# Graph-network kernel on one core: the first chunk's one-hot matrices built gather by gather, and the second chunk begun in half columns

## The chip, the cores and the metric

The kernel runs on one core of one Trainium2 chip. The metric is the device time of one execution, in microseconds; the kernel before takes 249.6 us (median of 3 runs, 249.52 to 250.2). The profiled execution is a fourth run with a time of its own.

## The reference, cut to what matters

1250 nodes with 512 features, 21250 edges sorted by destination. What the change touches is the first sum over neighbours (`segment_sum`); all that follows reads its result.

```
agg = jax.ops.segment_sum(x[src], dst, num_segments=N)
h = (1.0 + eps) * x + agg                      # first graph layer
h = relu(batch_norm(h @ W1 + b1, g1, be1))
h = relu(batch_norm(h @ W2 + b2, g2, be2))
x = layernorm(x + (x + h))
h = relu(x @ lW1 + lb1) @ lW2 + lb2            # second graph layer
x = layernorm(x + (h + segment_sum(h[col], row)))
```

## The kernel before

**Tiling.** The sum over neighbours is a matrix product with a count matrix `AT` (source node on the partitions, in 10 tiles `k` of 128 rows; destination node along 1250 columns). Features stand in 4 tiles `d` of 128. The columns are cut into three chunks `CH`: 0 to 250, 250 to 750 and 750 to 1250. A *unit* `(i, k)` is the pair of matmuls that adds source tile `k` of feature tile `d` to chunk `c` (`i = 4 c + d`): one for the high part `xh` of x, one for the remainder `xl = x - xh`, 250 columns wide in the first chunk and 500 in the others. A result `i` stays in PSUM bank `2 + i % 6` until ten units have gone into it.

**How AT is made.** Edges are packed as `dst * 1280 + src` (`pair`, VectorE), written to DRAM (`pairs`) and read back by two indirect DMAs that GpSimd issues one after the other: `run0` holds for each of 125 windows of 10 nodes the edges of its first five nodes, `run1` those of its last five. Where each window begins is its rank, found from `below` and `edge_row` on VectorE and four matmuls. VectorE subtracts the window's base (`rel`), TensorE transposes (L1182), and VectorE splits the result in `keyT` (source tile and node) and `loT` (source row in the tile). From these it makes, for each of 25 *groups* `g` of 50 columns, two one-hot matrices `hot_s` and `hot_k` (`one_hots`, L849 and L852, two buffers each). TensorE multiplies them in `build(g)` (ten matmuls of 50 columns, L1200, banks 0 and 1), and ScalarE copies the bank to `AT` (`group_out`, L569). `build(g)` needs the one-hots of g and the copy of g-2; the one-hots of g need `build(g-2)` done.

**The order of work.** Every engine runs an order written out by hand and waits on semaphores. The first five groups (`EARLY`) come ahead of everything; then groups 5 to 24 are *slots*: in slot g TensorE runs `build(g)` and the units that `slot_units[g]` lists (four in each). Slots 5 to 14 hold the 40 units of the first chunk, slots 15 to 24 the 40 of the second; the third chunk's 40 (`tail_units`) follow. Tables tell in which slot an engine does other things, on VectorE and ScalarE behind the one-hots or the copy of that slot:
- `cols_at` (TensorE): transposes of x tile k (`x_cols`), four matmuls. `turn_at` (ScalarE): their copy to `xT` (`x_turn`).
- `high_at` (ScalarE): `xh` of tile k (`x_high`, L565). `low_at` (VectorE): `xl` of tile k (`x_low`, L828), which waits for that `xh`.
- For a result that is done, VectorE adds `(1 + eps) x` two slots later (`h0_own`, L863), ScalarE rounds it three slots later (`h0_high`), and VectorE takes the remainder five slots later (`h0_low`, L870).

`between(n)` issues n matmuls of 256 columns whose result nobody reads.

## Time and profile before

| | before |
|---|---|
| Time, median of 3 runs | 249.6 us (249.52 to 250.2) |
| Time of the profiled execution | 249.95 us |
| Its span in the profile | 248.1 us |
| TensorE (PE) matmuls busy | 231.0 us, 93% of the span |
| VectorE (DVE) busy | 156.2 us, 63% |
| ScalarE (ACT) busy | 134.2 us, 54% |
| GpSimd (POOL) busy | 88.0 us, 35% |
| Chain that ended last | PE 70%, DVE 12%, DMA 7%, ACT 6% |

The span is what the engines' records cover, and 1.85 us of the profiled execution's time lie around it. A row of a timeline gives the start from the beginning of the span, the length, the engine, the line of the kernel and the operation. The start of the next row can lie ahead of the end of this one, since instructions of an engine overlap at their edges. So the cost of an instruction in a full queue is the distance from its start to the next start.

### The profile page before, as it was taken

Reading aid. Unit: us, or ns where it says so; the run is one execution under the profiler, and the core shown is the slowest. Engines: PE = TensorE matmul, PEld = TensorE weight load, DVE = VectorE, ACT = ScalarE, POOL = GpSimd, SP = SyncE. Lnnn points to the kernel's source line nnn. Section 1 sums busy time; section 2 is a strip of 40 time slices with the busy share of each in tenths; the row PEclk is TensorE's granted clock in tenths of the full one; section 3 lists DMA queues with packets and bytes.
Section 4 is the critical chain, followed back from the end, with each engine's and each line's share of the span. In section 5 each row is a group of like instructions: output and inputs, shape, how many; then the busy total and the mean of one; then the engine's idle time right before and its main releaser. Section 6 shows DMA issues by size and latency. Waiting matters only on the chain.

```text
span 248.1 us, 3897 instructions
## 1 busy us (share of the span) xinstructions
PE 231.0 (93%) x1454; PEld 197.3 (80%) x1454; DVE 156.2 (63%) x362; ACT 134.2 (54%) x233; POOL 88.0 (35%) x83
## 2 busy tenths in 40 slices
PE   0858999999999999999999999999999999999990
PEld 0845997777888888888888888888889997888970
DVE  1669899873966344555544316264876899796374
ACT  0656774763868067444455504457471639936373
POOL 5420000004920006565554500423456459701251
PEclk9999999999999999999999999999999999999998
DMA  3467800000066501111000087503209920000334
GB/s 100 156 214 214 202 0 3 1 3 3 3 261 239 198 1 45 42 42 45 0 0 0 4 206 142 106 3 60 45 4 170 202 85 3 0 0 0 131 127 160
DMA packets 32323, 19.96 MB, mean 80 GB/s; under 512 B 21927, under 2 KB 27084, under 8 KB 32302
## 3 DMA queue, kind: packets, MB, share of 16 engines
q1 hardware_dynamic: 31796, 19.45, 28.6%
q8 instruction: 13, 0.21, 0.4%
q0 software_dynamic: 160, 0.13, 0.2%
q10 hardware_dynamic: 346, 0.10, 0.2%
q14 instruction: 8, 0.07, 0.1%
HBM read 8.51 MB, written 5.92 MB: 58 GB/s over the span
## 4 chain that ended last, share of the span: by engine, by line
PE 70%; DVE 12%; DMA 7%; ACT 6%; issue 2%; POOL 1%; SPq 1%; DVEq 0%
PE ps L1281 22%; PE ps L1220 17%; PE ps L1298 11%; PE ps L1344 9%; PE ps L1362 6%; PE ps L1311 3%; DVE hot_s L849 3%; DMA plane_T<-planes 2%; PE ps L1200 2%; DMA src_i<-in_src 2%; DVE xT L984 2%; DMA pairs<-pair 2%; ACT planes L715 1%; DVE small_t L942 1%; DMA run<-pairs,start_i 1%
## 5 line engine op out<-in xcount | busy, mean ns | idle before, releaser
L942 DVE BATCH_NORM_STATS2 small_t<-ps 128x6 f32<-128x500 f32 (+1 forms) x36 | 21.6, 599 | 38.7 <-PE ps L1281 25.2
L1220 PE MATMUL ps<-AT,xh 128*128 128x500 f32 (+2 forms) x120 | 42.6, 366 | 0.4 <-ACT AT L569 0.4
L1220 PE MATMUL ps<-AT,xl 128*128 128x500 f32 (+2 forms) x120 | 40.9, 352 | 0.0
L1281 PE MATMUL ps<-h0h,wh 128*128 128x500 f32 (+1 forms) x96 | 33.9, 353 | 0.0
L1281 PE MATMUL ps<-h0h,wl 128*128 128x500 f32 (+1 forms) x96 | 33.9, 353 | 0.0
L1281 PE MATMUL ps<-h0l,wh 128*128 128x500 f32 (+1 forms) x96 | 33.8, 352 | 0.0
L485 POOL TENSOR_TENSOR wl<-w2s,wh 128x512 fp32r<-128x512 f32 x8 | 11.1, 1384 | 43.9 <-ACT wh L689 43.9
L480 POOL TENSOR_TENSOR wl<-w1s,wh 128x512 fp32r<-128x512 f32 x8 | 10.1, 1301 | 45.7 <-ACT AT L569 45.7
L1220 PEld LDWEIGHTS ps<-AT,xh 128*128 128x128 f32 (+1 forms) x120 | 22.6, 188 | 3.3 <-ACT AT L569 0.6
L1220 PEld LDWEIGHTS ps<-AT,xl 128*128 128x128 f32 (+1 forms) x120 | 22.7, 189 | 2.7
L1298 PE MATMUL ps<-a1h,wh 128*128 128x500 f32 (+1 forms) x96 | 23.7, 355 | 0.0
L1298 PE MATMUL ps<-a1h,wl 128*128 128x500 f32 (+1 forms) x96 | 23.5, 353 | 0.0
L1298 PE MATMUL ps<-a1l,wh 128*128 128x500 f32 (+1 forms) x96 | 23.4, 353 | 0.0
L569 ACT ACTIVATE AT<-ps 128x500 fp32r<-128x500 f32 x25 | 14.8, 590 | 15.6 <-PE ps L1200 15.6
L849 DVE TENSOR_TENSOR hot_s<-iota,loT 128x1280 bf16<-128x1280 bf16 x25 | 20.5, 820 | 2.3 <-PE ps L1200 2.2
L1344 PE MATMUL ps<-A,uh 128*128 128x512 f32 (+3 forms) x60 | 20.5, 357 | 0.0
L1281 PEld LDWEIGHTS ps<-h0h,wh 128*128 128x128 f32 x96 | 18.1, 188 | 2.9 <-issue 0.4
L1344 PE MATMUL ps<-A,ul 128*128 128x512 f32 (+3 forms) x60 | 20.3, 354 | 0.0
L1281 PEld LDWEIGHTS ps<-h0l,wh 128*128 128x128 f32 x96 | 18.0, 188 | 2.5
L1281 PEld LDWEIGHTS ps<-h0h,wl 128*128 128x128 f32 x96 | 18.0, 188 | 2.4
L489 POOL TENSOR_TENSOR a1l<-a,a1h 128x1250 fp32r<-128x1250 f32 x7 | 18.8, 2682 | 0.0
L663 ACT ACTIVATE small_t<-small_t 128x1 f32<-128x1 f32 x12 | 3.5, 295 | 27.7 <-DVE small_t L943 27.7
(148 smaller groups left out, 508.2 us busy)
## 6 DMA issues: line engine op xcount, KB each, us to landing
turns<-half_out SPq DMA_DIRECT2D x10, 320.0 KB, 2.2
out<-x SPq DMA_DIRECT2D x9, 256.0 KB
w1s<-in_L_gnn_W SPq DMA_DIRECT2D x4, 512.0 KB, 7.1
w2s<-in_L_gnn_W SPq DMA_DIRECT2D x8, 256.0 KB, 2.7
xs<-in_x SPq DMA_DIRECT2D x1, 1280.0 KB, 7.9
xs<-in_x SPq DMA_DIRECT2D x1, 1024.0 KB
lws<-in_L_gnn_W SPq DMA_DIRECT2D x1, 512.0 KB, 4.0
lw2s<-in_L_gnn_W SPq DMA_DIRECT2D x1, 512.0 KB, 4.2
```

What stands on the lines that cost most here:

```text
L480: nc.gpsimd.tensor_tensor(wl[:, t, :], w1s[:, t, :], wh[:, t, :].bitcast(F32), ALU.subtract).then_inc(w1l_set, 1)
L485: nc.gpsimd.tensor_tensor(wl[:, t, :], w2s[t % W2R][:, :], wh[:, t, :].bitcast(F32), ALU.subtract).then_inc(w2l_set, 1)
L489: nc.gpsimd.tensor_tensor(a1(a1l, t), a32[t % 2][:, :], a1(a1h, t).bitcast(F32), ALU.subtract).then_inc(a1l_set, 1)
L569: nc.scalar.activation(AT[:, :, g * WG * WIN:(g + 1) * WG * WIN].rearrange("p k (w d) -> p k w d", w=WG), ps[:, g % 2, 0:GCOLS].rearrange( ...
L849: nc.vector.tensor_tensor(hot_s[g % 2][:, :, :, :], iota2[:, None, :, :].broadcast_to([P, WG, P, 2]), loT[:, w, None, :].broadcast_to([P, ...
L942: link(nc.vector.bn_stats(stats[:, 6 * c:6 * c + 6], ps[:, zbank(t, c), 0:c1 - c0]))
L1220: last = mm(o, part[0:r, k, d * P:d * P + P], AT[0:r, k, c0:c1], start=(k == 0 and j == 0), stop=(k == NT - 1 and j == 1))
L1281: last = mm(ps[:, zbank(t, c), 0:c1 - c0], w[:, t, d * P:d * P + P], h[c][:, d, :], start=(d == 0 and j == 0), stop=(d == DT - 1 and j == 2))
L1298: last = mm(ps[:, zbank(t, c), 0:c1 - c0], w[:, k, (t - HT) * P:(t - HT + 1) * P], a1(a, k)[:, c0:c1], start=(k == 0 and j == 0), stop=(k ...
L1311: last = mm(u_at(k), x[:, d, P * k:P * k + r], w[:, d, :], start=(d == 0 and j == 0 and k % 2 == 0), stop=(d == DT - 1 and j == 2), skip_g ...
L1344: last = mm(v_at(i, m), (uh, ul)[j][0:r, k, m * P:m * P + P], a_rows(k)[0:r, c0:c1], start=(k == 0 and j == 0 and (m == 0 or v_banks[i][0] ...
L1362: last = mm(ps[0:r, y_banks[k % len(y_banks)], :], part[:, f:f + r], w[:, m, :], start=(m == 0 and j == 0), stop=(m == LT - 1 and j == 2))
```

## The change

- **Gather by gather.** The first chunk's 25 windows are no longer made into one-hots window by window, but half window by half window: flat views `keyW` and `loW` hold first the 25 half windows of `run0`, then the 25 of `run1`. Groups 0 and 1, and half of group 2, need only `run0`. Only the 25 columns of the first chunk are split at first (`early_keys`); the other 100 of each gather come behind the one-hots of group 4 (`late_keys`). The transposes go to free places in banks 2 and 7 (`keys_at`), and `early_out` copies to `AT` by half windows (group 2 in two copies).
- **Half columns.** Slots 5 to 10 hold five units of the first chunk each, slots 11 to 14 hold 3, 3, 2 and 2 and beside them five units each of `left`: the second chunk's first two feature tiles in their first 250 columns. Slots 15 to 19 then hold the other 250 columns of those (four units each), slots 20 to 24 the last two feature tiles in all 500 columns.
- **Ranks ahead of packing.** `below` and `edge_row` stand ahead of `pair` on VectorE.
- **x remainders with the pairs.** The copy `par` and the first five `x_low` behind it wait for `pair_out`, which the write of `pairs` gives.
- **Tables.** The x tiles move: only tile 5 is transposed ahead of slot 5 (it was 5 and 6), tiles 6 to 9 in slots 5 to 8; `high_at` and `low_at` are earlier too.

```diff
+        HALF_COLS = CH[0][1]
+        HALF_READY = (CH[1][0] + HALF_COLS) // (WG * WIN)
+        SPLIT = RING - DT
+        first = [(d, k, None) for k in range(NT) for d in range(DT)]
+        left = [(DT + d, k, 0) for k in range(NT) for d in range(SPLIT)]
+        second_units = [(DT + d, k, 1) for d in range(SPLIT) for k in range(NT)]
+        second_units += [(DT + d, k, None) for d in range(SPLIT, DT) for k in range(NT)]
...
+        first_per, left_per = [5] * 6 + [3, 3, 2, 2], [0] * 6 + [5] * 4
...
-        cols_at = {6: half + 2, 7: half + 3, 11: half + 4}
-        turn_at = {6: half + 2, 7: half + 3, 12: half + 4}
-        high_at = {5: half, 8: half + 1, 9: half + 2, 10: half + 3, 11: half + 4}
-        low_at = {7: half, 10: half + 1, 11: half + 2, 12: half + 3, 13: half + 4}
-        early_cols = {EARLY - 3: half, EARLY - 1: half + 1}
+        cols_at = {5: half + 1, 6: half + 2, 7: half + 3, 8: half + 4}
+        turn_at = dict(cols_at)
+        high_at = {5: half, 6: half + 1, 7: half + 2, 8: half + 3, 9: half + 4}
+        low_at = {6: half, 8: half + 1, 9: half + 2, 10: half + 3, 11: half + 4}
+        early_cols = {EARLY - 2: half}
...
+            v.wait_ge(pair_out, 16)
             nc.vector.tensor_copy(par[:, :], ps[:, 2, 0:3 * BT]).then_inc(par_set, 1)
...
+            def early_keys(c):
+                v.wait_ge(rel_T, c + 1)
+                f = slice(c * WE, (c + 1) * WE)
+                link(split(keyW[:, f], loW[:, f], keys_at(c, 0, WE)))
+
+            def late_keys(c):
+                split(keyT[:, WE:NW, c], loT[:, WE:NW, c], keys_at(c, WE, NW)).then_inc(keys_read, 1)
...
-            for g in range(EARLY):
-                one_hots(g)
...
+            shifted(0)
+            early_keys(0)
+            early_hots(0)
+            shifted(1)
+            early_hots(1)
+            early_keys(1)
+            early_hots(2)
+            early_hots(3)
+            v.wait_ge(counted, 1)
+            nc.vector.tensor_scalar(flag[0:1, :], ps[0:1, 2, 0:1], float(-2 * E), None,
+                                    ALU.not_equal).then_inc(flag_set, 1)
+            early_hots(4)
+            late_keys(0)
+            late_keys(1)
...
+                v.wait_ge(keys_read, 2)
                 for g in range(EARLY, NG):
                     one_hots(g)
...
+            keys(0)
+            pe.wait_ge(xT_set, fill_bank - 2)
+            between(8)
+            build(0)
+            keys(1)
+            between(3)
+            build(1)
+            count()
+            between(4)
+            build(2)
+            between(4)
+            build(3)
+            x_cols(early_cols[3])
+            build(4)
```

VectorE, from the landing of the first gather, before: both gathers are split in full (125 columns) and the first one-hots stand behind them.

```order
L838 TENSOR_SCALAR rel<-run_112,small_t 125x128
L841 TENSOR_SCALAR keyT<-ps 128x125
L842 SCALAR_TENSOR_TENSOR loT<-ps,keyT 128x125
L838 TENSOR_SCALAR rel<-run_113,small_t 125x128
L841 TENSOR_SCALAR keyT<-ps 128x125
L842 SCALAR_TENSOR_TENSOR loT<-ps,keyT 128x125
L849 TENSOR_TENSOR hot_s_69<-iota_120,loT 128x1280
L852 TENSOR_TENSOR hot_k_71<-iota_k,keyT 128x500
L849 TENSOR_TENSOR hot_s_70<-iota_120,loT 128x1280
L852 TENSOR_TENSOR hot_k_72<-iota_k,keyT 128x500
```

And now:

```order
L872 TENSOR_SCALAR rel<-run_112,small_t 125x128
L876 TENSOR_SCALAR keyT<-ps 128x25
L877 SCALAR_TENSOR_TENSOR loT<-ps,keyT 128x25
L893 TENSOR_TENSOR hot_s_69<-iota_120,loT 128x1280
L896 TENSOR_TENSOR hot_k_71<-iota_k,keyT 128x500
L872 TENSOR_SCALAR rel<-run_113,small_t 125x128
L893 TENSOR_TENSOR hot_s_70<-iota_120,loT 128x1280
L896 TENSOR_TENSOR hot_k_72<-iota_k,keyT 128x500
L876 TENSOR_SCALAR keyT<-ps 128x25
L877 SCALAR_TENSOR_TENSOR loT<-ps,keyT 128x25
L893 TENSOR_TENSOR hot_s_69<-iota_120,loT 128x1280
L896 TENSOR_TENSOR hot_k_71<-iota_k,keyT 128x500
```

The one-hots of group 0 moved ahead of the second gather's `rel`, and the splits are 25 columns wide.

VectorE behind the early groups, before (the first row is the one-hot of group 5; `xl` is that of tile 5):

```order
L849 TENSOR_TENSOR hot_s_70<-iota_120,loT 128x1280
L852 TENSOR_TENSOR hot_k_72<-iota_k,keyT 128x500
L849 TENSOR_TENSOR hot_s_69<-iota_120,loT 128x1280
L852 TENSOR_TENSOR hot_k_71<-iota_k,keyT 128x500
L849 TENSOR_TENSOR hot_s_70<-iota_120,loT 128x1280
L852 TENSOR_TENSOR hot_k_72<-iota_k,keyT 128x500
L828 TENSOR_TENSOR xl<-xs,xh 128x512
L849 TENSOR_TENSOR hot_s_69<-iota_120,loT 128x1280
```

And now:

```order
L904 TENSOR_TENSOR hot_s_70<-iota_120,loT 128x1280
L907 TENSOR_TENSOR hot_k_72<-iota_k,keyT 128x500
L904 TENSOR_TENSOR hot_s_69<-iota_120,loT 128x1280
L907 TENSOR_TENSOR hot_k_71<-iota_k,keyT 128x500
L863 TENSOR_TENSOR xl<-xs,xh 128x512
L904 TENSOR_TENSOR hot_s_70<-iota_120,loT 128x1280
L907 TENSOR_TENSOR hot_k_72<-iota_k,keyT 128x500
```

The remainder of tile 5 moved from behind group 7 to behind group 6, so that it stands ahead of group 7.

ScalarE in slot 5 and behind it, before (its first row is the copy of group 5):

```order
L569 ACTIVATE AT<-ps 128x10x50
L565 ACTIVATE xh<-xs 128x512
L569 ACTIVATE AT<-ps 128x10x50
L577 ACTIVATE xT<-ps 128x4x128
L569 ACTIVATE AT<-ps 128x10x50
L577 ACTIVATE xT<-ps 128x4x128
```

And now:

```order
L603 ACTIVATE AT<-ps 128x10x50
L611 ACTIVATE xT<-ps 128x4x128
L590 ACTIVATE xh<-xs 128x512
L603 ACTIVATE AT<-ps 128x10x50
L611 ACTIVATE xT<-ps 128x4x128
L590 ACTIVATE xh<-xs 128x512
```

The turned copy of tile 6 now stands between the copy of group 5 and `xh` of tile 5.

VectorE in slots 18 to 20 of the kernel now (the first row is the one-hot of group 18; `h0l_63` is a remainder of the first chunk, four in all, and the row with 128x500 is `h0_own` of the second chunk's first result):

```order
L904 TENSOR_TENSOR hot_s_69<-iota_120,loT 128x1280
L907 TENSOR_TENSOR hot_k_71<-iota_k,keyT 128x500
L925 TENSOR_TENSOR h0l_63<-ps,h0h_60 128x250 x2
L904 TENSOR_TENSOR hot_s_70<-iota_120,loT 128x1280
L907 TENSOR_TENSOR hot_k_72<-iota_k,keyT 128x500
L918 SCALAR_TENSOR_TENSOR ps<-xT,small_t,ps 128x500
L925 TENSOR_TENSOR h0l_63<-ps,h0h_60 128x250 x2
L904 TENSOR_TENSOR hot_s_69<-iota_120,loT 128x1280
L907 TENSOR_TENSOR hot_k_71<-iota_k,keyT 128x500
```

Before, all four remainders stood together behind group 19 (the first row) and behind `h0_own`:

```order
L849 TENSOR_TENSOR hot_s_70<-iota_120,loT 128x1280
L852 TENSOR_TENSOR hot_k_72<-iota_k,keyT 128x500
L863 SCALAR_TENSOR_TENSOR ps<-xT,small_t,ps 128x500
L870 TENSOR_TENSOR h0l_63<-ps,h0h_60 128x250 x4
L849 TENSOR_TENSOR hot_s_69<-iota_120,loT 128x1280
L852 TENSOR_TENSOR hot_k_71<-iota_k,keyT 128x500
```

The amount of this work is the same; what changed is that slots 15 to 19, beside it, hold units of 250 columns in place of 500.

## Rows read from the trace of the kernel before

**Rows 1.** Busy time by stretch: stretch, length, busy time of each engine, PEclk, DMA.
```profile
24.05:39.04 14.99, 14.68 (x202) 14.07 (x203) 14.30 (x26) 10.02 (x19) 0.00 (x0) 1.00 0.39 97
```
**Rows 2.** The chain that ended last, 5 to 42 us: start, length, what.
```profile
5.65 0.35 DVE pair L809
...
6.02 3.88 DMA pairs<-pair
...
12.40 3.41 DMA run<-pairs,start_i
...
22.81 0.45 PE ps L1200 x10
...
23.29 0.60 ACT AT L569
...
24.10 1.17 PE ps L1220 x8
...
26.82 0.44 PE ps L1162 x4
27.26 0.26 PE ps L1200 x10
27.52 1.02 PE ps L1220 x8
...
41.39 1.90 PE ps L1220 x8
```
**Rows 3.** Timeline of GpSimd, 10 to 14 us: start, length, instruction, idle before.
```profile
10.22 1.88 POOL L472 DMA_INDIRECT run<-pairs,start_i  x1 [2.20 <-DMA pairs<-pair]
12.40 1.30 POOL L472 DMA_INDIRECT run<-pairs,start_i  x1 [0.31 <-issue]
```
**Rows 4.** Timeline of VectorE, 14 to 23 us: start, length, instruction, idle before.
```profile
14.21 0.29 DVE L838 TENSOR_SCALAR rel<-run,small_t 125x128 f32<-125x128 f32 x1 [0.98 <-DMA run<-pairs,start_i]
14.98 0.30 DVE L841 TENSOR_SCALAR keyT<-ps 128x125 bf16<-128x125 f32 x1 [0.49 <-PE ps L1182]
15.32 0.30 DVE L842 SCALAR_TENSOR_TENSOR loT<-ps,keyT 128x125 bf16<-128x125 f32 x1
...
17.29 0.83 DVE L849 TENSOR_TENSOR hot_s<-iota,loT 128x1280 bf16<-128x1280 bf16 x1
18.03 0.41 DVE L852 TENSOR_TENSOR hot_k<-iota_k,keyT 128x500 bf16<-128x500 bf16 x1
...
22.71 0.83 DVE L849 TENSOR_TENSOR hot_s<-iota,loT 128x1280 bf16<-128x1280 bf16 x1
```
**Rows 5.** Timeline of TensorE, 28 to 50 us.
```profile
28.39 0.60 PE L1162 MATMUL ps<-ident,xs 128*128 128x128 f32 x4
...
37.47 0.43 PE L1200 MATMUL ps<-hot_k,hot_s 128*128 128x50 bf16 x10 [0.22 <-DVE hot_k L852]
...
49.65 0.44 PE L1200 MATMUL ps<-hot_k,hot_s 128*128 128x50 bf16 x10
```
**Rows 6.** Timeline of ScalarE, 25 to 30 us.
```profile
25.59 0.59 ACT L569 ACTIVATE AT<-ps 128x500 fp32r<-128x500 f32 x1 [1.22 <-PE ps L1200]
26.07 0.63 ACT L565 ACTIVATE xh<-xs 128x512 fp32r<-128x512 f32 x1
...
29.02 0.60 ACT L577 ACTIVATE xT<-ps 128x512 f32<-128x512 f32 x1 [0.65 <-PE ps L1162]
```
**Rows 7.** Timeline of VectorE, 26 to 47 us.
```profile
26.73 0.69 DVE L828 TENSOR_TENSOR xl<-xs,xh 128x512 fp32r<-128x512 f32 x1
27.34 0.82 DVE L849 TENSOR_TENSOR hot_s<-iota,loT 128x1280 bf16<-128x1280 bf16 x1
...
44.67 0.74 DVE L863 SCALAR_TENSOR_TENSOR ps<-xT,small_t,ps 128x500 f32<-128x500 f32 x1
45.32 1.39 DVE L870 TENSOR_TENSOR h0l<-ps,h0h 128x250 fp32r<-128x250 f32 x4
46.62 0.82 DVE L849 TENSOR_TENSOR hot_s<-iota,loT 128x1280 bf16<-128x1280 bf16 x1
```

126 lines of the change are left out of this document (77 added, 49 removed).

## The prediction

> **What bounds the kernel now.** I read the busy times by stretch first, then the chain of waits, then the timelines of three engines beside each other. From 24.05 to 39.04 us, the slots of the first chunk, TensorE's matmuls are busy 14.68 of 14.99 us and VectorE 14.30, at a granted clock of 1.00 (the 2.4 GHz level) [rows 1]. So two engines are nearly full there, and whatever one of them waits for shows in the other. Ahead of 24 us TensorE is fed through one chain [rows 2]: pairs packed at 5.65, written (3.88 us), gathered (the second gather lands at about 15.8), split, made into one-hots for five groups, `build(4)` at 22.81, the copy to `AT` at 23.29, first unit at 24.10. From then on TensorE seldom waits: the first chunk's forty units, ten builds and three sets of transposes are 10 x (1.02 + 0.27) + 2 x 0.44 + 0.34 (tile 9 has 98 rows, so 98 columns of 128) = 14.1 us [rows 2], and `build(15)` comes 14.67 us after 24.10 (39.04 less a build of 0.27), so 0.57 us of waits for one-hots lie in between, of which one stands in front of `build(14)` at 37.47 [rows 5]. A good mark is `build(20)`, at 49.65 [rows 5]: by then kernel before and now have done the same units (first chunk, and the first two results of the second), and behind it both run the same work in the same order. What `build(20)` shifts by, the end shifts by, since the rest hangs on TensorE and on what TensorE ends.
>
> **The start: 1.1 us won.** *Ranks ahead of packing.* `pair` began at 5.65, when the sources had landed [rows 2]; `below` and `edge_row` fit between the destinations' landing and that. `pair` stays at 5.65 and so do the write and the gathers, which wait for it. The ranks were not what the gather waited for: it is issued at 10.22, after the write landed at 9.90 (6.02 + 3.88) [rows 2, 3]. I cost this edit at nothing (0.05 either way). The wait of `par` and `x_low` for the write is over at 9.90, when x has only just come; nothing too.
>
> *Gather by gather.* `rel` of the first gather stands at 14.21 and its first split at 14.98, after the transpose [rows 4]. A split of 125 columns takes 0.34 to the next start. No row shows 25 columns: between 0 and 0.34; a remainder of 512 columns takes 0.69 and a split of 125 takes 0.30 [rows 4, 7], about 1 ns a column, so I take 0.22. The one-hots cost 0.74 + 0.33 = 1.07 a group (17.29 to 18.03, and five groups with the flag in 5.42 up to 22.71) [rows 4]. So group 0 starts at 14.98 + 0.44 = 15.42, the second `rel` (0.25) at 16.49, group 1 at 16.74, the second split (0.44) at 17.81, group 2 at 18.25, group 4 with the flag (0.06) at 20.45, its end 1.15 later at 21.60, `build(4)` at 21.7 in place of 22.81. That is 1.1 earlier (0.6 if the narrow splits cost as much as wide ones, 2.0 if they cost nothing; by the rows' 1 ns a column neither end is likely), and the first unit comes at 23.0. ScalarE's two sign sums wait for the second `rel` and then hold group 0's copy until about 17.9; the next builds come at 18 and 19.5, so that hides.
>
> *What it pushes back.* The four splits of 100 columns now stand behind group 4: from 21.6, near 0.3 each, so group 5's one-hots start at 22.8, as late as before (22.71 [rows 4]). The lead of 1.1 is TensorE's alone; VectorE has none from here.
>
> **Slots 5 and 6: a new wait of 1.14 us.** Each step is a duration from a row.
> - First unit 23.0; ten matmuls of 250 columns. Eight take 1.02, eight of 500 take 1.90 [rows 2], so one of 250 is between 0.11 (the difference by eight) and 0.128; I take 0.117, and ten make 1.26. `build(5)` at 24.26, transposes of tile 6 at 24.53, `build(6)` when its one-hots are there: 22.8 + 1.07 + 1.20 = 25.07 (0.10 of wait). Then units to 26.60, transposes of tile 7 to 27.04: TensorE is ready for `build(7)`.
> - ScalarE: copy of group 5 at 24.74 (a copy starts 0.48 behind its build, 22.81 to 23.29 [rows 2]). Then, new here, the turned copy of tile 6: its transposes are seen 0.63 after their start (28.39 to 29.02 [rows 5, 6]), so at 25.16, and ScalarE is free at 25.22. Only then `xh` of tile 5, at 25.72.
> - VectorE: `xl` of tile 5 follows `xh` by 0.66 (26.07 to 26.73 [rows 6, 7]), so at 26.38. VectorE was ready for it at 22.8 + 2.14 = 24.94 and stands still for 1.4 us, with group 7's one-hots queued behind it. They start 0.61 later [rows 7], at 26.99, and end 1.15 later: `build(7)` at 28.18.
> TensorE waits 1.14 us. Before, `xl` of tile 5 stood behind group 7 and `xh` right behind the copy of group 5, and `xl` started without idle time [rows 7].
>
> **Slots 7 to 20.** From 28.18: two slots of five units with transposes (1.97 and 1.87), two without (1.53 each), two of eight units (0.27 + 1.96), two of seven (0.27 + 1.72): `build(15)` at 43.5. VectorE needs 1.07 a slot and 0.6 for a remainder, so it catches up and the old 0.57 of waits goes. Slots 15 to 19 now take 1.29 each, `build(20)` would be at 49.99. But VectorE has more than 1.29 to do there: from `build(16)` at 44.8 its group 18 starts at 45.3; then 1.07, two remainders of the first chunk 0.65 (four take 1.30, 45.32 to 46.62), group 19 1.07, one `h0_own` 0.65 (44.67 to 45.32), two more remainders 0.65 [rows 7]: group 20 starts at 49.39 and is done 1.20 later. `build(20)` at 50.6: 0.60 of wait. At 500 columns a slot took 2.17 (0.27 + 1.90) and this was covered.
>
> **The sum at `build(20)`.** Start -1.10; tile 6's transposes, once in the idle start, now in the full stretch +0.44; twenty units in halves (40 more matmuls of 0.117, less 5 x (1.90 - 1.02)) +0.30; old waits -0.57; new waits 0.10 + 1.14 + 0.60 = +1.84. Together +0.91, from 49.65 to about 50.6. The profiled execution took 249.95 us and its span 248.1; the median of the runs shown is 249.6. I add 0.9 to the median: 250.5 us.
>
> **The rivals.**
> - *The stall is there but smaller, and slots 15 to 19 are covered.* If `xl` waits half as long (0.57 less) the sum is +0.3; if instead only the 0.60 is missing, also +0.3: 249.9, no change that can be told. For it: both waits end a chain of five or six steps, each read to 0.05. Against it: VectorE's order is fixed and it is ready 1.4 us early. 0.23.
> - *The first gather is issued faster.* GpSimd's first issue took 1.88 us, its second 1.30 [rows 3]; the first had VectorE's remainders beside it. If the wait for the write took these out of its way, everything up to the first unit would come up to 0.58 earlier: +0.3, 249.9. Against it: the wait ends at 9.90, before the issue at 10.22, so the same remainders run beside the same issue. 0.08. The Trainium skill (GPSIMD Engine Reference, section Specifications) says that GpSimd shares its SBUF interfaces with VectorE and that instructions with two SBUF inputs contend; by that rule the slower first issue is contention, and this kernel keeps it; the trace shows the two lengths, not their cause.
> - *Faster.* The stall at `xl` of tile 5 doesn't reach TensorE. It decides at `xh`: were it seen on VectorE by 25.2, `build(7)` would be met at 27.04, and the sum is -0.2; with slots 15 to 19 covered as well it is -0.8, 248.8. For it: the gain at the start is real and TensorE has units enough. Against it: the turned copy stands ahead of `xh` in ScalarE's order, 0.5 that nothing can pass. 0.16.
> - *The start isn't won.* A group among the first waits for something else (the sign sums on ScalarE, the narrow transposes), and the first unit stays at 24.1: the sum is then about +2.0, less what VectorE catches up meanwhile, 251.3. 0.07.
> - The forecast, 250.1 to 251.0 with the two waits as worked out: 0.46.
>
> The Trainium skill (VectorE: DVE Perf Modes, section The TRN2 errata) says that a Vector instruction pays a fixed cost beside its columns, 120 cycles of 0.96 GHz with PSUM as the source, so that cutting work in small pieces costs. By it a split of 25 columns is an estimated 0.15 us and one of 125 0.26, where the trace has 0.30 for the latter [rows 4]; with 0.15 in place of 0.22 four narrow splits would win 0.3 more at the start.
>
> **How the numbers follow.** A median of three runs tells about 0.3% (0.75 us) from no change. The forecast of +0.9 lies just beyond it: of its 0.46, 0.36 is slower and 0.10 the same; the start not won adds 0.07 to slower; the two rivals at +0.3 give 0.31, of which 0.03 might still be slower; "faster" 0.16, of which only 0.13 passes 0.3%. Slower 0.46, same 0.40, faster 0.14. The range 249.0 to 251.3 leaves out the full gain (the best of the faster case) and the worst of the lost start.
>
> **What would show it.** `build(4)` at 21.7 and the first unit at 23.0 (start); idle time of over 1 us on VectorE ahead of `xl` of tile 5, released by ScalarE's `xh`, and over 1 us on TensorE ahead of `build(7)`; no idle time from slot 8 to 19; about 0.6 ahead of `build(20)`, which stands at 50.6. Wrong it is if `build(7)` starts before 27.5, or if `build(4)` comes before 21.3 or after 22.2.

## The result, and the profile after

The changed kernel takes 252.88 us, the median of five runs (252.84 to 253.29), against 250.2 us for five runs of the kernel before on the same chip: a ratio of 1.0119, 95% interval 1.0101 to 1.0137. It is slower by 1.2%. The prediction was 250.5 us with a range of 249.0 to 251.3. The sign was right; the size was not, and the range missed it: +0.9 was forecast, and the medians are 2.68 us apart. The profiled execution is the slowest of the five, 253.29 us (before 249.95), so 3.34 us have to be found in the trace.

The start comes nearly as forecast. This is VectorE's timeline of the changed kernel; the columns are those of [rows 4].
```profile
14.40 0.29 DVE L872 TENSOR_SCALAR rel<-run,small_t 125x128 f32<-125x128 f32 x1 [1.11 <-DMA run<-pairs,start_i]
15.32 0.19 DVE L876 TENSOR_SCALAR keyT<-ps 128x25 bf16<-128x25 f32 x1 [0.63 <-PE ps L1247]
15.54 0.19 DVE L877 SCALAR_TENSOR_TENSOR loT<-ps,keyT 128x25 bf16<-128x25 f32 x1
15.76 0.83 DVE L893 TENSOR_TENSOR hot_s<-iota,loT 128x1280 bf16<-128x1280 bf16 x1
...
22.56 0.28 DVE L877 SCALAR_TENSOR_TENSOR loT<-ps,keyT 128x100 bf16<-128x100 f32 x1
23.63 0.83 DVE L904 TENSOR_TENSOR hot_s<-iota,loT 128x1280 bf16<-128x1280 bf16 x1 [0.79 <-DVE loT L877]
...
26.94 0.69 DVE L863 TENSOR_TENSOR xl<-xs,xh 128x512 fp32r<-128x512 f32 x1 [1.09 <-ACT xh L590]
27.55 0.82 DVE L904 TENSOR_TENSOR hot_s<-iota,loT 128x1280 bf16<-128x1280 bf16 x1
```
The narrow splits cost 0.22 us from start to start, the value taken, and 0.19 by themselves, so the 0.15 that the prediction also considered is too low. Further down stands the first thing that was not forecast: group 5's one-hots start at 23.63, not at 22.8, behind 0.79 us of idle time that the profile puts down to an instruction long finished. The last line but one is the forecast stall: VectorE stands idle 1.09 us ahead of the remainder of tile 5, until ScalarE's `xh` is there.

ScalarE's timeline at the same place, with the turned copy of tile 6 ahead of `xh`, as worked out (compare [rows 6]):
```profile
25.32 0.59 ACT L603 ACTIVATE AT<-ps 128x500 fp32r<-128x500 f32 x1 [1.81 <-PE ps L1267]
25.80 0.59 ACT L611 ACTIVATE xT<-ps 128x512 f32<-128x512 f32 x1
26.28 0.62 ACT L590 ACTIVATE xh<-xs 128x512 fp32r<-128x512 f32 x1
```

TensorE's timeline has the marks that [rows 2, 5] have for before: builds 4, 7, 20 and 24, the first unit, and the end of the slots.
```profile
21.92 0.44 PE L1267 MATMUL ps<-hot_k,hot_s 128*128 128x50 bf16 x10 [0.16 <-DVE hot_k L896]
23.26 0.35 PE L1293 MATMUL ps<-AT,xh 128*128 128x250 f32 x1 [0.90 <-ACT AT L595]
...
28.75 0.44 PE L1267 MATMUL ps<-hot_k,hot_s 128*128 128x50 bf16 x10 [0.72 <-DVE hot_k L907]
...
51.10 0.43 PE L1267 MATMUL ps<-hot_k,hot_s 128*128 128x50 bf16 x10 [0.41 <-DVE hot_k L907]
...
59.80 0.44 PE L1267 MATMUL ps<-hot_k,hot_s 128*128 128x50 bf16 x10
...
61.76 0.38 PE L1293 MATMUL ps<-AT,xl 98*128 98x500 f32 x1
63.87 0.47 PE L1293 MATMUL ps<-AT,xh 128*128 128x500 f32 x1 [1.73 <-DVE h0l L925]
```
`build(20)` stands 1.45 us later than before (forecast 0.95, from 49.65 to 50.6). The larger part comes behind it, where the forecast had nothing. The kernel before went from its last unit of the second chunk into the third without a gap. Here are its `build(24)`, its last matmul of the second chunk and its first of the third:
```profile
58.36 0.44 PE L1200 MATMUL ps<-hot_k,hot_s 128*128 128x50 bf16 x10
...
60.32 0.39 PE L1220 MATMUL ps<-AT,xl 98*128 98x500 f32 x1
60.55 0.39 PE L1220 MATMUL ps<-AT,xh 128*128 128x500 f32 x1
```
From 60.32 to 60.55 is 0.23 us; from 61.76 to 63.87 is 2.11. The profile names VectorE's `h0l` as what ended the gap, and the chain of waits of the changed kernel follows it there (start, length, what):
```profile
60.24 1.92 PE ps L1293 x8
62.16 0.02 issue
62.18 0.74 DVE ps L918
62.93 0.59 DVE h0l L925
63.52 0.35 issue
63.87 2.28 PE ps L1293 x9
```
But between the last unit of slot 24 and the first of the third chunk the code has one more thing, which is no busy time and so stands in no timeline: the end of the `with pe.If` block, a jump over the `Else` block. Asked for that line by itself, the trace of the changed kernel and the trace of before say (number of executions; shortest, median and longest in ns; start of the first and the last):
```profile
L1315 PEldq COMPARE_BRANCH  x2: 88/1983/3878, 22.9 to 59.8; - x2
```
```profile
L1235 PEldq COMPARE_BRANCH  x2: 88/252/417, 23.9 to 58.4; - x2
```
The jump took 3.88 us in place of 0.42. So there were two theories of the 1.9 us. *Fetch:* the sequencer, which reads TensorE's instructions, has to fetch some that it did not fetch ahead; the `Else` block had grown with the half columns. *Buffer:* the third chunk's first unit waits for a PSUM bank that VectorE's `h0l` gives back late.

### The profile page after: what moved, and what is told of

Same layout as the page of the kernel before. It is cut to its first block, busy times and chain, and to the rows that moved or that the text cites. A ratio compares the mean times of both kernels' runs of the same rounds, so it can differ in the third digit from the quotient of the medians.

```text
span 251.5 us, 3979 instructions
## 1 busy us (share of the span) xinstructions
PE 233.1 (93%) x1492; PEld 200.6 (80%) x1492; DVE 156.7 (62%) x366; ACT 134.1 (53%) x234; POOL 87.9 (35%) x83
## 3 DMA queue, kind: packets, MB, share of 16 engines
HBM read 8.51 MB, written 5.92 MB: 57 GB/s over the span
## 4 chain that ended last, share of the span: by engine, by line
PE 81%; DVE 10%; DMA 5%; ACT 2%; issue 1%; DVEq 0%; ACTq 0%
PE ps L1378 22%; PE ps L1361 22%; PE ps L1293 16%; PE ps L1424 9%; PE ps L1442 6%; PE ps L1391 3%; PE ps L1267 2%; DMA run<-pairs,start_i 2%; DMA dst_i<-in_dst 2%; DVE hot_s L904 2%; DVE hot_s L893 2%; DMA pairs<-pair 2%; DVE h0l L925 1%; DVE small_t L1006 1%; ACT xr L692 1%
## 5 line engine op out<-in xcount | busy, mean ns | idle before, releaser
L1293 PE MATMUL ps<-AT,xh 128*128 128x250 f32 (+3 forms) x140 | 44.4, 339 | 2.6 <-DVE h0l L925 1.7
L1293 PE MATMUL ps<-AT,xl 128*128 128x250 f32 (+3 forms) x140 | 42.7, 326 | 0.0
L1293 PEld LDWEIGHTS ps<-AT,xh 128*128 128x128 f32 (+1 forms) x140 | 26.4, 188 | 5.2 <-issue 2.1
L1293 PEld LDWEIGHTS ps<-AT,xl 128*128 128x128 f32 (+1 forms) x140 | 26.5, 189 | 2.1
L603 ACT ACTIVATE AT<-ps 128x500 fp32r<-128x500 f32 x20 | 11.9, 595 | 13.4 <-PE ps L1267 13.3
L904 DVE TENSOR_TENSOR hot_s<-iota,loT 128x1280 bf16<-128x1280 bf16 x20 | 16.4, 822 | 2.6 <-PE ps L1267 1.5
```

Of the source, the lines that this page charges most:

```text
L603: nc.scalar.activation(AT[:, :, g * WG * WIN:(g + 1) * WG * WIN].rearrange("p k (w d) -> p k w d", w=WG), ps[:, g % 2, 0:GCOLS].rearrange( ...
L904: nc.vector.tensor_tensor(hot_s[g % 2][:, :, :, :], iota2[:, None, :, :].broadcast_to([P, WG, P, 2]), loT[:, w, None, :].broadcast_to([P, ...
L1293: last = mm(o, part[0:r, k, d * P:d * P + P], AT[0:r, k, c0 + p0:c0 + p1], start=(k == 0 and j == 0 and h != 1), stop=(k == NT - 1 and j = ...
```

## The experiments

Fourteen kernels ran. All times are medians; the ratio, with its interval, is that to the kernel before on the same chip. The changed kernel did not run again beside them, so a difference in microseconds to its 252.88 is one between chips, and the ratios are the fairer comparison. "Tail" is the third chunk's first matmul. A `...` in a diff marks lines left out.

**Which theory of the jump.** Three kernels change nothing but the `Else` block, of the changed kernel or of the kernel before.

*short_else:* 40 whole units in place of 60 in the `Else` block.
```diff
-                for u in first + left + second_units:
+                for u in first + whole_units:
```


> The changed kernel, but in the branch that is never taken with these inputs TensorE's second chunk stands in whole units: 40 matmuls fewer to jump over. What runs is the same instructions in the same order. In the changed kernel TensorE's compare-and-branch behind slot 24 lasts 3.88 us (0.42 before), a 16 KB packet of the instruction queue falls into it, and the first unit of the third chunk starts 1.73 us late. Theory A (the jump lands on instructions that have not been fetched): with a shorter jump the branch lasts about 0.4 us, the third chunk starts at about 62.0 and the time falls by 1.8 us, from 252.9 to about 251.1; it can also stay, if the target still lies beyond what is there. Theory B (the wait is what the profile names, a remainder on VectorE that frees a PSUM bank): nothing changes, since the order of the remainders is the same; 252.9.

Measured: 252.59 us, 1.0093 (1.0064 to 1.0122). The jump took 3.79 us and the tail came 2.03 behind the last unit. Shortening the block by 80 instructions did not help.

*before_long_else:* the reverse, on the kernel before.
```diff
-                for u in units[0:(len(CH) - 1) * per]:
+                for u in units[0:per]:
                     aggregate(*u)
+                for d in range(DT):
+                    for h in ((0, 1) if d < 2 else (None,)):
+                        for k in range(NT):
+                            part_unit(DT + d, k, h)
...
```
(`part_unit` is a unit as the changed kernel has it, whole or half.)

> The kernel before, with 40 matmuls more in the branch that is never taken (the second chunk's first two results in half columns). What runs is unchanged. Theory A: the branch behind slot 24 lasts 3 to 4 us in place of 0.42 if the longer jump leaves what is fetched, and the time rises by 1.8 us to about 252.0; since the jump starts elsewhere than in the changed kernel it may just still land inside, and then nothing changes. Theory B: nothing changes, 250.2.

Measured: 251.82 us, 1.0077 (1.0051 to 1.0102). Nothing that is executed differs from the kernel before, and it is 1.8 us slower. (In the profiled execution 0.30 of that lies ahead of the jump, `build(24)` at 58.66: the granted clock was 0.50 from 16 to 22 us then. From `build(24)` to the first matmul of the next stage it takes 21.76 us, before 20.39.) This is its line of the jump, and its timeline at the tail, where the profile now blames no engine:
```profile
L1254 PEldq COMPARE_BRANCH  x2: 88/1697/3306, 24.1 to 58.7; - x2
```
```profile
60.62 0.38 PE L1220 MATMUL ps<-AT,xl 98*128 98x500 f32 x1
62.16 0.47 PE L1220 MATMUL ps<-AT,xh 128*128 128x500 f32 x1 [1.16 <-issue]
```
That refutes the buffer theory: code that never runs makes the gap.

*else_cut:* the changed kernel, with the second chunk's units left out of the branch not taken.
```diff
-                for u in first + left + second_units:
+                for u in first:
```


> The changed kernel; it leaves out, in TensorE's branch not taken, the whole second chunk's units, so that the jump over it skips 231 TensorE instructions instead of 475. Everything executed is the same. Both forms of the fetch theory: the branch behind slot 24 lasts about 0.4 us, the tail follows, 251.1 us (1.8 under the changed kernel). Buffer theory: no difference, 252.9 us, with the tail's gap at about 1.7 us.

Measured: 251.04 us, 1.0034 (1.0022 to 1.0045): 1.84 us under the changed kernel, as expected (0.85% by the ratios). The tail follows its unit after 0.23 us, and the line of the jump reads
```profile
L1315 PEldq COMPARE_BRANCH  x2: 88/204/319, 22.5 to 59.5; - x2
```

**Length or position?** The kernel before skips 386 instructions cheaply and short_else 395 dearly, which could be a limit of length. The Trainium skill (Runtime: NRT & Kernel Launch, section Instruction fetch mechanics) says that instructions come in blocks of 16 KiB, 256 instructions, fetched in sequence, and that a taken branch whose target isn't in the current window of two pages has to wait for a fetch. By that rule it is the position that counts, and a jump of 395 can be made cheap by instructions put in ahead of it. The trace shows packets of 16384 bytes on the instruction queue, one of them inside the changed kernel's jump (61.37 us).

*short_filled:* short_else and 276 waits for counts already reached (the program packs two to an instruction, 138 in all).
```diff
+            def filler(n, least):
+                for _ in range(n):
+                    pe.wait_ge(const, least)
+
+            filler(190, 0)
             pe.wait_ge(rowsel, 1)
...
```


> The changed kernel with the second chunk's units of the branch not taken written as 40 whole units (as in the run with the shortened branch), and with 135 instructions put in ahead of the jump that only wait for a count already reached: 95 before TensorE's first matmul, 27 before the first turned run, 8 each before builds 2 and 3, all where TensorE was idle. The result is the same. It tells two forms of the fetch theory apart from one that looks only at the length of the jump. Position theory: a jump is cheap if its target lies in the 256-instruction stretch in use or the next one; counting the program's TensorE instructions, the jump now stands at 200 of its stretch instead of 62, and the same 395 skipped instructions end in the next stretch: the branch behind slot 24 takes about 0.4 us, the tail follows without a gap of more than 0.2, and the time is about 1.8 us under the changed kernel's, 251.1 us. Length theory (395 instructions are too far wherever they stand, 386 are not): branch 3.3 to 3.9 us, time 252.5 to 252.9 us. Buffer theory (the tail waits for h0's low part): the same as the length theory's.

Measured: 254.28 us, 1.0166 (1.0144 to 1.0189). The time was missed by 3.2 us for a reason of its own: a filling instruction costs 0.1 us, not the 0.05 that its own record shows. The 95 ahead of the first matmul fill 0.8 to 11.06 us, and that matmul comes at 11.06 instead of 5.92. The question put was answered all the same: the tail follows after 0.23 us, and from `build(24)` to the first matmul of the next stage it is 20.40 us (changed kernel 22.36, before 20.39). Length is not it. The jump itself is on record with 1.42 us, which the matmuls still in the array's queue covered.

For each kernel I counted TensorE's instructions in the program (a matmul counts two, its weights and itself): S is the jump's place, modulo 256, and D how many it skips. (The instructions that the traces show ahead of the jump give the same differences in S between all sixteen kernels.)

| kernels | S | D | jump, us | last unit to tail, us |
|---|---|---|---|---|
| before | 240 | 386 | 0.42 | no gap (0.23) |
| before_long_else | 240 | 468 | 3.31 | 1.54 |
| changed, late_keys_behind, xlow_group7, ranks_back, no_pair_wait | 62 | 475 | 3.30 to 3.88 | 1.53 to 2.11 |
| short_else | 62 | 395 | 3.79 | 2.03 |
| else_cut, best_cut | 62 | 231 | 0.32 | no gap (0.23) |
| short_filled, best_filled | 200 | 395 | 1.42, 1.66 | no gap (0.23) |
| start_only, whole_units | 238 | 395 | 1.24, 0.42 | no gap (0.23) |
| best_nofill | 25 | 395 | 0.32 | no gap (0.23) |
| one_split | 22 | 395 | 0.42 | no gap (0.23) |

With an offset o for where the blocks' edges lie, "the target is in the block in use or in the next", (S + o) mod 256 + D under 512, fits all sixteen kernels for o from 60 to 91, and no limit on D alone fits them. Where the rule makes a jump dear, TensorE stands idle for 1.3 to 1.9 us (the last column less 0.23); the sequencer's branch is longer than that, since the array works off its queue meanwhile: the changed kernel's jump begins at 59.8, and matmuls that were already queued start until 61.76.

The instruction queue itself shows what a long jump waits for. Taken from the traces: the last packet of 16384 bytes on that queue to land before the jump's end.

| kernel | packet's start, from the jump's start, us | it takes, us | jump, us | jump's end behind the landing, us |
|---|---|---|---|---|
| changed | 1.55 | 0.96 | 3.88 | 1.37 |
| ranks_back | 1.00 | 1.32 | 3.68 | 1.36 |
| late_keys_behind | 0.97 | 0.97 | 3.30 | 1.36 |
| short_filled | -1.03 | 1.09 | 1.42 | 1.35 |
| best_filled | -1.03 | 1.32 | 1.66 | 1.37 |
| start_only | -1.15 | 0.98 | 1.24 | 1.40 |
| before | -3.12 | 0.92 | 0.42 | 2.62 |

All ten jumps of over 1.2 us end 1.35 to 1.40 us behind such a landing; the six of 0.32 to 0.42 us end 2.1 us or more behind the last one and wait for none. So a dear jump waits for a packet that starts only about 1.0 to 1.5 us after the jump has begun. Its 3.3 to 3.9 us follow from when that packet starts and how long it takes, and the jumps of 1.2 to 1.7 us met one that was already under way.

**The stall at build 7, and VectorE's late start.**

*xlow_group7:* tile 5's remainder one slot later, as it was before.
```diff
-        low_at = {6: half, 8: half + 1, 9: half + 2, 10: half + 3, 11: half + 4}
+        low_at = {7: half, 8: half + 1, 9: half + 2, 10: half + 3, 11: half + 4}
```


> The changed kernel with the remainder of x tile 5 back behind the one-hots of group 7 (one number in the table). Theory A (VectorE stands still 1.1 us for xh of tile 5, and build 7 is late for that): build 7 at 27.85 in place of 28.75, no idle time ahead of it, 0.9 us faster, and build 20 still waits 0.4 to 0.6 us. Theory B (the slots are bound by TensorE's own work and the wait is made up for later): the same time.

Measured: 251.67 us, 1.0068 (1.0043 to 1.0093). TensorE no longer waits at `build(7)`:
```profile
27.30 0.60 PE L1228 MATMUL ps<-ident,xs 128*128 128x128 f32 x4
27.74 0.42 PE L1267 MATMUL ps<-hot_k,hot_s 128*128 128x50 bf16 x10
```
What this one entry is worth depends on the mark it is read from. From `build(4)` to `build(24)` it takes 36.58 us in place of 37.88, 1.30 less. But `build(4)` came late in this execution: 5.48 us behind VectorE's second `rel` (16.70), where the changed kernel has 5.08 (from 16.84), and VectorE's own instructions did not wait for it. The granted clock was 0.50 from 20 to 22.2 us, as it was in late_keys_behind; here is that stretch in late_keys_behind and then in else_cut (stretch, length, busy times, and PEclk as the third from the end):
```profile
20.00:22.20 2.20, 2.20 (x24) 1.87 (x22) 2.17 (x8) 1.33 (x3) 0.00 (x0) 0.50 0.22 72
20.00:22.20 2.20, 1.61 (x27) 1.00 (x24) 2.14 (x8) 1.34 (x4) 0.00 (x0) 1.00 0.22 70
```
Read from the second `rel`, `build(7)` comes after 11.04 us in place of 11.91 and `build(24)` after 42.06 in place of 42.96: the entry is worth 0.9. In the changed kernel and in four others with its start and its tables (short_else, else_cut, ranks_back, no_pair_wait) that distance to `build(7)` is 11.91 to 11.93.

*late_keys_behind:* the four late splits behind VectorE's own branch.
```diff
-            late_keys(0)
-            late_keys(1)
             v.wait_ge(flag_set, 1)
             bad = v.value_load(flag[0:1, 0:1], min_val=0, max_val=1)
+            links = n[0]
             with v.If(bad == 0):
+                late_keys(0)
+                late_keys(1)
                 v.wait_ge(keys_read, 2)
...
```


> The changed kernel with VectorE's four late splits moved behind its branch. In the changed kernel VectorE loads the flag at 22.58, behind the splits, and the one-hots of group 5 start at 23.63, 0.79 us after the last split ends; before, the same load and branch (about 1.0 us) lay beside the one-hots of group 4. Theory A (the branch costs 1 us from when the sequencer comes to it, and the splits uncovered it): group 5's one-hots start at 22.9, build 5 at 24.5 in place of 24.84, build 7 at 28.4 in place of 28.75, as the wait for the x remainder takes up the rest; 0.3 us faster. Theory B (the late splits themselves hold group 5, their wait on PSUM reads or on the semaphore): group 5 stays at 23.6 and the time the same.

Measured: 252.54 us, 1.0099 (1.0075 to 1.0123). The idle time ahead of group 5 is gone:
```profile
22.48 0.27 DVE L877 SCALAR_TENSOR_TENSOR loT<-ps,keyT 128x100 bf16<-128x100 f32 x1
22.78 0.83 DVE L904 TENSOR_TENSOR hot_s<-iota,loT 128x1280 bf16<-128x1280 bf16 x1
```
Group 5 now starts at 22.78, where the prediction had it. On the path it won nothing in this execution: `build(7)` stands at 28.73 (changed kernel 28.75), and `build(24)` at 59.78 (59.80). From `build(4)` to `build(24)` it is 0.28 less, but `build(4)` itself was 0.26 late (22.18 in place of 21.92), at the granted clock of 0.50; that the 0.28 would be won with a `build(4)` in time isn't shown. In time the difference to the changed kernel (0.34) lies within the intervals. What the move is worth shows once the stall at tile 5 is gone too, in best_cut below.

**The two parts costed at nothing.**

*ranks_back:* the packed pairs ahead of the ranks again.
```diff
+            v.wait_ge(src_in, 16)
+            nc.vector.scalar_tensor_tensor(out=pair[0:ER, :], in0=dst_i[0:ER, :], scalar=float(STEP),
+                                           in1=src_i[0:ER, :], op0=ALU.mult, op1=ALU.add).then_inc(pair_set, 1)
             link(nc.vector.tensor_scalar(below[0:ER, :], win_row[0:ER, :], dst_f[0:ER, EC - 1:EC], None, ALU.is_gt))
```


> The changed kernel with the packed pairs put ahead of the ranks again on VectorE, as before. My prediction gave this part nothing: 252.9 us, within 0.3, first gather issued at 10.2 to 10.3 us either way, build 4 at 21.9 within 0.2. Rival: the pairs are what the gathers wait for, so the first gather comes 0.2 us earlier and the time falls by as much, 252.6. It also shows whether the 8 filling matmuls at 15 us take 0.24 us each because TensorE did nothing before 5.9 us and had gaps, or whatever the order: by the first, TensorE's early work moves by 0.2 us only and they stay at 0.24.

*no_pair_wait:* the wait ahead of `par` taken out.
```diff
             v.wait_ge(par_T, 1)
-            v.wait_ge(pair_out, 16)
```


> The changed kernel without VectorE's wait for the pairs' way out ahead of par and the x remainders, as before. My prediction gave the wait nothing: the first gather's index is written before it and the DMA of the pairs has long landed. 252.9 us within 0.3, and build 4 at 21.7 to 21.9. Rival: the remainders run earlier and free 0.2 to 0.4 us on VectorE ahead of the first shift, which waits for the gather anyway, so nothing follows; or VectorE and the gather's descriptors on GpSimd disturb each other as the wait may be meant to prevent, the first gather lands 0.3 us later, and the time is 253.2.

Measured: 252.74 us, 1.0101 (1.0078 to 1.0124), and 252.51 us, 1.0091 (1.0071 to 1.0111). GpSimd's first issue in the changed kernel, in ranks_back and in no_pair_wait, from the three timelines:
```profile
10.29 1.88 POOL L496 DMA_INDIRECT run<-pairs,start_i  x1 [3.17 <-DMA pairs<-pair]
```
```profile
10.21 1.88 POOL L496 DMA_INDIRECT run<-pairs,start_i  x1 [2.24 <-DMA pairs<-pair]
```
```profile
10.20 1.77 POOL L496 DMA_INDIRECT run<-pairs,start_i  x1 [3.18 <-DMA pairs<-pair]
```
The ranks are worth nothing that shows. The wait neither costs nor gains anything: without it the first `rel` stands at 14.19 and `build(24)` at 59.45, and in else_cut, which has it, at 14.20 and 59.46. So the first issue still takes 1.88 us with the wait, and the rival's gain of up to 0.58 us isn't there. The ranks' place isn't what slows the eight filling matmuls at 15 us either: they took 1.92 us in ranks_back, 1.91 in the changed kernel, and 1.04 in else_cut, which has the changed kernel's order.

**Putting the findings together.** *best_filled* and *best_cut* have three moves in common: the two edits above, and the first chunk's four remainders of h0 one to a slot.
```diff
+        FIRST_LOW = {18: [0], 19: [1], 20: [2], 21: [3]}
+
+        def low_after(g):
+            return FIRST_LOW.get(g, []) + [i for i in h0_after(g - LOW_LAG) if i >= DT]
...
```
best_filled has the filling instructions of short_filled besides, best_cut the cut `Else` of else_cut. So else_cut and best_cut are no complete kernels: with inputs that take the `Else` branch they would leave out the second chunk.

> What the runs so far point to, put together, with the same result: the changed kernel with the jump brought to a cheap place as in the run short_filled (about -1.8 us against the changed kernel), the late keys behind VectorE's branch (-0.3), tile 5's x remainder in slot 7 rather than 6 (-1.1), and the first chunk's four remainders of h0 one to a slot in slots 18 to 21 instead of two in 18 and two in 19 (build 20 no longer waits for VectorE, 0.4 to 0.6 off the path). Sum about -3.6: 249.2 us, range 248.7 to 250.0, against 250.1 for the kernel before. If the jump stays dear, 251.0.

> The same kernel as best_filled without the filling instructions; in their place it leaves out, in TensorE's branch not taken, the second chunk's units, so that the jump skips 231 instructions. Everything executed is the same as in the changed kernel but for three moves: the late keys behind VectorE's branch, tile 5's remainder in slot 7, the first chunk's remainders of h0 in slots 18, 19, 20 and 21. The run with the cut branch alone measured 251.0; the three moves should add -0.3, -1.1 and -0.5: 249.2 us, 248.7 to 249.7. In best_filled, build 24 stood 35.6 us behind build 4 (changed kernel 37.9), so if build 4 is at 21.7 here, build 24 should be at 57.3 and the first Z matmul at 77.7. If the gains of best_filled hung on its late start, build 24 stands at 58.5 or later.

Measured: best_filled 252.37 us, 1.0134 (1.0064 to 1.0204; one of its four runs took 255.6), spoiled by the filling as short_filled was. best_cut 248.43 us, 0.9935 (0.9916 to 0.9953), faster than the kernel before by 0.65%. Its `build(4)` stands 5.09 us behind the second `rel`, as in the changed kernel, so here the distance from `build(4)` to `build(24)` can be compared: 35.72 in place of 37.88, 2.16 less for the three moves. From `build(4)` to `build(7)` it is 5.25 in place of 6.83. Of these 1.58 us tile 5's remainder alone gave 0.88, so the late splits give 0.7 beside it. (This shares out the 1.58; the late splits alone, with a granted clock of 1.00, were not run.) The other 0.58 is the wait at `build(20)` (forecast 0.60), which has gone:
```profile
48.04 0.28 PE L1301 MATMUL ps<-AT,xl 98*128 98x250 f32 x1
48.16 0.43 PE L1275 MATMUL ps<-hot_k,hot_s 128*128 128x50 bf16 x10
```

*best_nofill:* the three moves, a complete `Else`, and the 19 filling matmuls of the start left out.
```diff
             keys(0)
             pe.wait_ge(xT_set, fill_bank - 2)
-            between(8)
             build(0)
             keys(1)
-            between(3)
             build(1)
...
```


> The three moves of best_cut with a complete branch not taken (395 instructions skipped), and the 19 filling matmuls of the start left out (8, 3, 4 and 4, which write a bank that nobody reads), by which the jump stands 38 instructions earlier, at 25 of its stretch. From where the six jumps measured so far were cheap or dear, the stretches' edge lies so that this jump is cheap if the offset is under 92, and the times of the block fetches speak for an offset near 80. Two things are told: whether the jump is cheap (249.2 us as best_cut, branch 0.4 us) or dear (251.0, branch over 3 us); and what the filling matmuls are worth: if TensorE's clock falls without them, the builds and transposes before 22 us take twice as long, build 4 stands at 22.5 or later, and 0.6 us or more is lost.

Measured: 251.71 us, 1.0054 (1.0034 to 1.0073). The jump is cheap (0.32 us), as the position rule said. `build(4)` is hardly late (21.94; 22.5 or later was expected for a fallen clock); but 2.5 us are lost between `build(4)` and `build(7)`, 7.80 in place of 5.25. The first lines are best_nofill's timeline, the last its busy times by stretch:
```profile
24.95 0.41 PE L1302 MATMUL ps<-AT,xl 128*128 128x250 f32 x1
25.16 0.41 PE L1302 MATMUL ps<-AT,xh 128*128 128x250 f32 x1
...
29.06 0.28 PE L1302 MATMUL ps<-AT,xh 128*128 128x250 f32 x1
29.18 0.28 PE L1302 MATMUL ps<-AT,xl 128*128 128x250 f32 x1
```
```profile
23.30:28.80 5.50, 5.50 (x40) 5.35 (x41) 3.31 (x7) 2.59 (x5) 0.00 (x0) 1.00 1.17 299
```
TensorE is busy through all of 23.30 to 28.80, the granted clock (third column from the end) is 1.00, and yet the 250-column matmuls follow each other in 0.21 us, 1.2 columns a ns, which is the 1.2 GHz level; from 29 on they follow in 0.12 us as in best_cut, 2.1 columns a ns, the 2.4 GHz level. Before 22 us, where the filling matmuls had stood, TensorE was busy 1.29 of the 4 us from 14 to 18 (best_cut 2.63). So leaving out the filling matmuls costs 2.5 us in this stretch, and the column of the granted clock doesn't show it.

*start_only:* the change's start alone: no half columns, four units a slot, the x tables of before but for tile 6, late splits behind the branch, complete `Else`.
```diff
-        first_per, left_per = [5] * 6 + [3, 3, 2, 2], [0] * 6 + [5] * 4
+        left, second_units = [], [(DT + d, k, None) for d in range(DT) for k in range(NT)]
+        first_per, left_per = [4] * 10, [0] * 10
-        high_at = {5: half, 6: half + 1, 7: half + 2, 8: half + 3, 9: half + 4}
-        low_at = {6: half, 8: half + 1, 9: half + 2, 10: half + 3, 11: half + 4}
+        high_at = {5: half, 8: half + 1, 9: half + 2, 10: half + 3, 11: half + 4}
+        low_at = {7: half, 10: half + 1, 11: half + 2, 12: half + 3, 13: half + 4}
...
```


> The change's start alone, with a complete branch not taken: first chunk's one-hots gather by gather, ranks ahead of packing, the early and late keys (the late ones behind VectorE's branch); no half columns, slots 5 to 14 with four whole units each, and the x tables of before, except that tile 6 is turned in slot 5. The jump stands at 238 of its stretch and skips 395 instructions, so that by the position theory it is cheap. Against the kernel before: build 4 at 21.7 to 21.9 instead of 22.8 (-1.0), tile 6's four transposes back in the path (+0.4): build 24 at 57.8 (58.4 before), no new gap at the tail, time 249.5 us, 249.0 to 249.9, against 250.3. By the length theory (395 too far) it would be 251.4. If the start's gain is lost again in slots 5 to 14 for another reason, 250.3.

Measured: 249.61 us, 0.9976 (0.9965 to 0.9986): 0.24% faster than before, near what the start less tile 6's transposes should give (-1.1 + 0.44 = -0.66; measured -0.48, and -0.44 at `build(24)`, 57.92 against 58.36).

**The half columns by themselves.**

*whole_units:* best_cut's tables and moves without half columns (`first_per` as in start_only, `low_at` with `{7: half, 8: half + 1, ...}`), complete `Else`.

> The changed kernel with the three moves of best_cut (late keys behind VectorE's branch, tile 5's remainder in slot 7, the first chunk's h0 remainders one to a slot) and its x tables, but without half columns: slots 5 to 14 have four whole units each, and the second chunk begins in slot 15. The branch not taken is complete; the jump stands at 238 and skips 395, where start_only's was cheap. Against best_cut (248.4; build 24 stood 35.7 us behind build 4) this takes away the half columns alone. By my prediction's term half columns cost 0.3 us, which would give 248.1 and build 24 at 35.4 behind build 4. Rival: they fill time in which TensorE waits in slots 5 to 14 for VectorE's one-hots (2.5 us a slot with four units against 1.3 us of TensorE work), so that without them slots 11 to 14 wait and slots 15 to 24 carry 40 whole units again: 36.3 behind build 4 as in start_only, 249.3 us.

Measured: 249.78 us, 0.9982 (0.9969 to 0.9995). `build(4)` to `build(24)` takes 36.71 us, best_cut's 35.72: taking the half columns away costs 0.99 us. The rival is right in its direction, and the loss is 0.4 us more than it said (36.3 and 249.3). Here are `build(9)`, `build(10)` and `build(11)` of whole_units, in slots without transposes, TensorE's timeline:
```profile
29.59 0.42 PE L1276 MATMUL ps<-hot_k,hot_s 128*128 128x50 bf16 x10
31.13 0.43 PE L1276 MATMUL ps<-hot_k,hot_s 128*128 128x50 bf16 x10
32.79 0.44 PE L1276 MATMUL ps<-hot_k,hot_s 128*128 128x50 bf16 x10 [0.23 <-DVE hot_k L913]
```
A slot of four units is 1.29 us of work, and these builds and `build(12)` stand 1.54, 1.66 and 1.67 apart: VectorE, with one-hots and a remainder of x in each of slots 7 to 11, sets the pace. From `build(12)` on, without remainders, it is 1.29 a slot. With five units a slot (1.53) TensorE has something to do in that time.

*one_split:* a complete kernel with half columns for one of the second chunk's four feature tiles, placed by the position rule before it was run.
```diff
-        SPLIT = RING - DT
+        SPLIT = 1
-        first_per, left_per = [5] * 6 + [3, 3, 2, 2], [0] * 6 + [5] * 4
+        first_per, left_per = [5] * 4 + [4] * 2 + [3] * 4, [0] * 6 + [3, 3, 2, 2]
...
```


> A complete kernel, made to beat both: the three moves of best_cut, and half columns for one 128-row piece of the second chunk instead of two (10 half units, three, three, two and two in slots 11 to 14; the first chunk's units five a slot in slots 5 to 8, four in 9 and 10, three in 11 to 14). That is 40 TensorE instructions fewer ahead of the jump, which then stands at 22 of its stretch and skips 395. Position theory: it ends in the next stretch (best_nofill's at 25 did), the branch takes 0.4 us and the tail follows at once: 248.8 us, 248.3 to 249.4. Length theory: 250.6. If the half columns pay, it lies between whole_units and best_cut.

Measured: 249.15 us, 0.9961 (0.9946 to 0.9976): faster than the kernel before (by 0.4%) and than the changed one, complete, and with a cheap jump:
```profile
L1324 PEldq COMPARE_BRANCH  x2: 88/252/417, 22.3 to 57.4; - x2
```

## Why the prediction was wrong

Step by step, forecast and the changed kernel's trace:

| step | forecast | trace |
|---|---|---|
| `build(4)` | 21.7 | 21.92 |
| `build(4)` to the first unit | 1.30 | 1.34 |
| first unit to `build(7)` | 5.18 | 5.49 |
| `build(7)` to `build(15)` | 15.3 | 15.30 (44.05 - 28.75) |
| `build(15)` to `build(20)` | 7.1 | 7.05 |
| `build(20)` against before | +0.95 | +1.45 |
| from `build(20)` to the first matmul of the next stage, against before | 0 | +1.96 |

**Right:** the ranks and the wait at nothing; the narrow splits at 0.22; the start won 0.89 of 1.10 in this execution (others had `build(4)` as early as 21.57 with the same start); the stall of VectorE at tile 5's remainder, with its cause and its place; the wait at `build(20)`, worth 0.58 (0.60); no wait between slots 8 and 19. Without the dear jump these steps give nearly the time forecast: else_cut is 0.73 us over the kernel before on its chip (+0.9 forecast). That is in part luck: in else_cut the start is 0.13 better than forecast and the way from the first unit to `build(7)` 0.39 worse.

**Wrong by 0.3:** "group 5's one-hots start at 22.8, as late as before". I had added up VectorE's instructions and left out what its sequencer does between them, reading the flag and branching. Before, that lay beside group 4's one-hots; in the changed kernel group 4 and the splits are queued in another order and it shows as 0.79 us of idle time. So `build(5)` came 1.58 us behind the first unit and not 1.26. The copy of group 5, `xh`, the remainder of tile 5 and `build(7)` follow it one after the other and kept the 0.32; that is the 0.31 in the third line of the table. The waits were also shared out otherwise than forecast: TensorE lost 0.32 ahead of `build(5)`, 0.36 ahead of `build(6)` (forecast 0.10) and 0.87 ahead of `build(7)` (forecast 1.14; 0.72 of it is idle time in the profile), read from start to start, less the forecast's times for the work between. The 0.87 is what xlow_group7 gives back (0.88).

**Wrong by 0.2:** `build(4)`. The gather landed 0.19 us later in this execution (`rel` at 14.40, before 14.21), which is no effect of the change: else_cut, with the same start, had it at 14.20 and `build(4)` at 21.57.

**Wrong by 1.96, the step that failed:** "What `build(20)` shifts by, the end shifts by", since both kernels "run the same work in the same order". They do, but not the same program: the change lengthened the `Else` block that the jump behind slot 24 skips (475 instructions, before 386) and moved the jump itself (62 of its block, before 240). I had taken everything in the diff that isn't executed as free. before_long_else shows the cost without the change (+1.8 us in the median, 1.37 of it behind `build(24)` in the trace), else_cut the change without the cost (-1.84), the kernels placed by the position rule agree, and the dear jumps end a fixed time after a packet of instructions lands.

**One term had its parts wrong though the sum held:** half columns +0.30 and old waits -0.57, together -0.27. whole_units against best_cut gives -0.99 for the halves with these x tables. The added matmuls do cost, but they fill slots in which TensorE would wait for VectorE; and with the x work drawn forward those waits are longer than the 0.57 read from before (1.0 from `build(9)` to `build(12)` of whole_units). The sum held because both terms describe the same slots: it is the halves that take the waits away. What I costed as a loss and a small gain is the one part of slots 5 to 20 that pays.

So the change is two good parts (the start, the half columns), two slips in its tables and the place of the late splits (2.2 us together), and a jump that got dear for a reason that stands in no line of the schedule (1.4 to 2.0 us behind `build(24)`, by execution). Without them it is best_cut, 248.4 us, of which about 0.4 us is a gather that landed earlier in its profiled execution.

## What to carry to other kernels

When a diff changes how many instructions an engine has, ahead of a jump or in the block that it skips, count them: a jump whose target lies beyond the next block of 256 instructions cost 1.3 to 1.9 us here, and a few dozen instructions more or less at either place turn it on or off. A gap right behind the end of an `If` isn't explained by the releaser that the profile names until the branch instruction's own duration has been read. Where an engine reads a register and branches in the middle of its work, count that too (0.79 us of idle time on VectorE here), in the order of the queue. And when two executions are compared from a mark on one engine, ask whether the other engines were just as late at that mark: here a late `build(4)` made two edits look 0.3 to 0.4 us better than VectorE's mark does.
